# Four-visit turns behind the woven visits of a graph-attention edge pass, with buffer counts in registers

## The reference, cut to what matters

```python
xl = x @ Wl.T + bl
xr = x @ Wr.T + br
e = edge_attr @ We.T
m = xl[src] + xr[dst] + e
score = jnp.where(m > 0, m, NEG_SLOPE * m) @ att
smax = jax.ops.segment_max(score, dst, num_segments=N)
es = jnp.exp(score - smax[dst])
denom = jax.ops.segment_sum(es, dst, num_segments=N)
out = jax.ops.segment_sum(alpha[:, None] * xl[src], dst, num_segments=N)   # alpha = es / denom[dst]
```

## Time and profile before

| what | value |
|---|---|
| three timed runs, us | 6142.74, 6151.49, 6149.81 |
| median, us | 6149.81 |
| the profiled execution, us | 6128.16 |
| its span, us | 6126.2 |
| TensorE matmul busy | 5403.3 us, 88% |
| VectorE busy | 4183.1 us, 68% |
| GpSimd busy | 3068.8 us, 50% |
| ScalarE busy | 2663.4 us, 43% |
| indirect gathers (line 701) | 3200 |
| matmuls of the weighted sum (line 976) | 6352 |

### The profile page before, as it was taken

One profiled execution on the slowest core, in us unless ns is written; L12 is line 12 of the kernel. 1 busy time (PEld: TensorE's weight loads), 2 busy tenths in 40 slices (PEclk: granted clock), 3 DMA queues, 4 the chain that ended last, 5 costly groups with the idle time before them and its releaser, 6 DMA issues. The chain is left out here.

```text
span 6126.2 us, 174836 instructions
## 1 busy us (share of the span) xinstructions
PE 5403.3 (88%) x41112; PEld 3782.6 (62%) x41113; DVE 4183.1 (68%) x13187; ACT 2663.4 (43%) x5435; POOL 3068.8 (50%) x3217
## 2 busy tenths in 40 slices
PE   0599999999999976999999999999688899995998
PEld 0466666666666655666666666666587333334988
DVE  5677777777777776777777777777623788885121
ACT  0244444444444433444444444444311688883010
POOL 0477777777777755777777777777300000000000
PEclk9899999999999988999999999999888999997999
DMA  1344444444444434444444444444184233332967
GB/s 50 84 108 107 109 110 109 109 106 104 108 107 110 109 68 102 110 110 109 110 110 104 105 109 110 110 110 109 42 330 184 90 114 105 119 101 113 381 251 302
DMA packets 708090, 771.75 MB, mean 126 GB/s; under 512 B 376370, under 2 KB 629401, under 8 KB 682913
## 3 DMA queue, kind: packets, MB, share of 16 engines
q1 hardware_dynamic: 560771, 578.84, 31.2%
q0 software_dynamic: 102400, 105.06, 9.3%
q10 hardware_dynamic: 44832, 86.76, 3.9%
HBM read 678.16 MB, written 88.81 MB: 125 GB/s over the span
## 5 line engine op out<-in xcount | busy, mean ns | idle before, releaser
L701 POOL DMA_INDIRECT gat_rows<-rows_scr,gat_idx x3200 | 3056.2, 955 | 1214.2 <-issue 1035.0
L853 ACT ACTIVATE gat_weightsT<-gat_tps 128x512 f32<-128x512 f32 x800 | 477.7, 597 | 1146.5 <-PE gat_tps L967 1130.9
L839 ACT ACTIVATE gat_weights<-gat_masked,gat_newtop 128x512 f32<-128x512 f32 x800 | 577.4, 722 | 864.0 <-DVE gat_newtop L799 668.0
L746 DVE TENSOR_SCALAR adj_hot_key<-adj_iota_key,adj_winbase,adj_key 128x392 bf16<-128x392 int16 x2416 | 951.4, 394 | 0.2 <-issue 0.2
L957 PE MATMUL gat_sps<-gat_relu,gat_att 128*128 128x256 f32 x3200 | 906.3, 406 | 0.0
L915 PE MATMUL gat_counts<-adj_hot_key,adj_hot_lo 128*128 128x392 bf16 x2416 | 724.5, 334 | 153.0 <-DVE adj_hot_key L746 61.2
L745 DVE TENSOR_SCALAR adj_hot_lo<-adj_iota_lo,adj_low 128x128 bf16<-128x128 int16 x2416 | 672.1, 278 | 206.1 <-issue 184.6
L976 PE MATMUL gat_aps<-gat_rows,gat_weightsT 128*128 128x65 f32 x6352 | 797.5, 269 | 0.0
L976 PEld LDWEIGHTS gat_aps<-gat_rows,gat_weightsT 128*128 128x128 f32 x6352 | 771.9, 192 | 0.0
L915 PEld LDWEIGHTS gat_counts<-adj_hot_key,adj_hot_lo 128*128 128x128 bf16 x2416 | 232.7, 96 | 685.3 <-DVE adj_hot_key L746 493.7
L957 PEld LDWEIGHTS gat_sps<-gat_relu,gat_att 128*128 128x128 f32 x3200 | 543.4, 189 | 178.7 <-issue 137.3
(11 more groups left out here) (336 smaller groups left out, 6807.9 us busy)
## 6 DMA issues: line engine op xcount, KB each, us to landing
gcn_sum_adj<-adj_scr SPq DMA_DIRECT2D x98, 1568.0 KB, 8.5
gat_dstb<-dst_scr SPq DMA_DIRECT2D x800, 128.0 KB
gat_ea<-in_ea SPq DMA_DIRECT2D x800, 128.0 KB
gin_sum_adj<-adj_scr SPq DMA_DIRECT2D x49, 1568.0 KB, 8.5
adj_scr<-adj_tiles ACTq DMA_DIRECT2D x48, 1568.0 KB
at_adj<-adj_scr SPq DMA_DIRECT2D x84, 896.0 KB
gat_rows<-rows_scr,gat_idx POOLq DMA_INDIRECT x3200
gat_xr<-xr_scr SPq DMA_DIRECT2D x1600, 24.0 KB
```

The source lines that it names most:

```text
L701: pool.indirect_dma_start(rows[:, u, c, 0:ROW], None, rows_d, bass.IndirectOffsetOnAxis(ap=idx[:, u, c:c + 1], axis=0)).then_inc(s_g[u], 16)
L746: dve.tensor_scalar(plan.hot_key[:, slot, :], plan.iota_key[:], plan.winbase[:, bass.ds(w, 1)], plan.key[:, bass.ds(c, 1)], ALU.add, ALU.i ...
L839: act.activation(wts[:, j, :], masked[:, j, :], ACT.Exp, bias=newtop[:, j:j + 1], scale=-1.0)
```

## The change

Behind the 392 woven visits, the work is done in turns of four visits, not eight. `turns_sb` now holds the number of these short turns, (visits + 4 + 3 - 392) >> 2. SyncE and GpSimd get a second loop for them, and all five engines loop over it. The ring of eight slots stays, so behind the woven visits only slots 0 to 3 are used, and the visit that held a slot before is eight back in the first short turn and four back in any later one. SyncE and GpSimd keep the count to wait for in a register (`freed`), which grows by eight after the first short turn and by four after later ones. TensorE's weighted sum lags by three visits, so in the first three visits of a short turn it reads a slot given by a register (`behind`): 5 to 7 in the first short turn, 1 to 3 in later ones. VectorE reads the destinations of a plain visit from a fixed slot.

```diff
@@ -47,6 +47,7 @@
 WOVEN = NW // 2 // RING
+TAIL = WOVEN * RING
@@ -376,12 +377,12 @@  (visit_list)
-            dve.tensor_scalar(turns_f[:, 0:1], ends[:, NGP - 1:NGP], float(DRAIN + RING - 1), None, ALU.add)
+            dve.tensor_scalar(turns_f[:, 0:1], ends[:, NGP - 1:NGP], float(DRAIN + TURN - 1 - TAIL), None, ALU.add)
...
-            dve.tensor_scalar(turns_sb[:], cols_i[:, 0:1], RING.bit_length() - 1, None, ALU.arith_shift_right)
+            dve.tensor_scalar(turns_sb[:], cols_i[:, 0:1], TURN.bit_length() - 1, None, ALU.arith_shift_right)
@@ -645,11 +646,14 @@  (SyncE)
-            turns = sp.value_load(turns_sb[0:1, 0:1], min_val=2, max_val=VTAB // RING)
+            tails = sp.value_load(turns_sb[0:1, 0:1], min_val=1, max_val=(VTAB - TAIL) // TURN)
...
-            with sp.Fori(1, turns) as i:
+            with sp.Fori(1, WOVEN) as i:
                 for u in range(RING):
                     load_pair(i, u)
                     sp.wait_ge(s["message"], count("message", i * RING + u, RING))
                     group_parts(u)
                     range_parts(u)
+            freed, gone = sp.alloc_register(tag + "_sp_freed"), sp.alloc_register(tag + "_sp_gone")
+            sp.reg_mov(freed, count("message", TAIL, RING))
+            sp.reg_mov(gone, RING)
+            with sp.Fori(0, tails) as i:
+                for u in range(TURN):
+                    load_pair_at(i * (TURN // 2) + TAIL // 2, u)
+                    sp.wait_ge(s["message"], sp.snap(freed, min_val=1, max_val=1 << 16) + u)
+                    group_parts(u)
+                    range_parts(u)
+                sp.reg_add(freed, freed, gone)
+                sp.reg_mov(gone, TURN)
@@ (GpSimd)
-            with pool.Fori(0, turns) as i:
+            def gather(summed, u, filled):
+                pool.wait_ge(s_id[u], filled * 32 + 32)
+                pool.sem_inc(s_loaded, 1)
+                pool.wait_ge(s["sum"], summed)
+                pool.nop(nofuse=True)
...
+            with pool.Fori(0, WOVEN) as i:
                 for u in range(RING):
...
+                    gather(count("sum", i * RING + u, RING), u, i)
+            freed, gone = pool.alloc_register(tag + "_pool_freed"), pool.alloc_register(tag + "_pool_gone")
+            pool.reg_mov(freed, count("sum", TAIL, RING))
+            pool.reg_mov(gone, RING)
+            with pool.Fori(0, tails) as i:
+                for u in range(TURN):
+                    gather(pool.snap(freed, min_val=1, max_val=1 << 16) + u, u, i + WOVEN)
+                pool.reg_add(freed, freed, gone)
+                pool.reg_mov(gone, TURN)
@@ (VectorE)
-                    near = dstb[:, bass.ds((i & 1) * TURN + u, 1), :].rearrange("p a e -> p (a e)")
+                    near = dstb[:, bass.ds((i & 1) * TURN + u, 1), :].rearrange("p a e -> p (a e)") if woven else dstb[:, u, :]
...
-            with dve.Fori(WOVEN * RING // TURN, dve.snap(turns * (RING // TURN), min_val=1)) as i:
-                turn(i, False)
+            with dve.Fori(0, tails) as i:
+                turn(i + TAIL // TURN, False)
@@ (ScalarE)
-            with act.Fori(WOVEN, turns) as i:
-                for u in range(RING):
-                    visit(i * RING + u, u)
+            with act.Fori(0, tails) as i:
+                for u in range(TURN):
+                    visit(i * TURN + (TAIL + u), u)
@@ (TensorE)
             def turn(i, woven, first=False):
-                for u in range(RING):
-                    step = i * RING + u
+                visits(i * RING, RING, i, woven, first)
+
+            def visits(first_step, many, filled, woven, first=False, back=None):
+                for u in range(many):
+                    step = first_step + u
...
-                    j, v = (u - 3) % 2, (u - 3) % RING
+                    j = (u - 3) % 2
+                    v = slice((u - 3) % RING, (u - 3) % RING + 1) if back is None or u >= 3 else bass.ds(back + u, 1)
...
                     for c in range(GC):
-                        last = pe.matmul(aps[:, 0:D + 1], wtsT[:, j, c * P:(c + 1) * P], rows[:, v, c, 0:D + 1],
+                        last = pe.matmul(aps[:, 0:D + 1], wtsT[:, j, c * P:(c + 1) * P],
+                                         rows[:, v, c, 0:D + 1].rearrange("p a f -> p (a f)"),
                                          start=(c == 0), stop=(c == GC - 1))
...
-            with pe.Fori(WOVEN, turns) as i:
-                turn(i, False)
+            behind = pe.alloc_register(tag + "_pe_behind")
+            pe.reg_mov(behind, RING - 3)
+            with pe.Fori(0, tails) as i:
+                visits(i * TURN + TAIL, TURN, i + WOVEN, False, back=pe.snap(behind, min_val=TURN - 3, max_val=RING - 3))
+                pe.reg_mov(behind, TURN - 3)
```

More of the change, by code:

```diff
@@ L647, in _, with load_pair_at @@
             half = [sp.alloc_register(f"{tag}_half{j}") for j in range(2)]
-            turns = sp.value_load(turns_sb[0:1, 0:1], min_val=2, max_val=VTAB // RING)
+            tails = sp.value_load(turns_sb[0:1, 0:1], min_val=1, max_val=(VTAB - TAIL) // TURN)
+            def load_pair_at(word, u):
+                if u % 2 == 0:
+                    sp.reg_load(pair, words[0:1, bass.ds(word + u // 2, 1)])
             def load_pair(i, u):
-                if u % 2 == 0:
-                    sp.reg_load(pair, words[0:1, bass.ds(i * (RING // 2) + u // 2, 1)])
+                load_pair_at(i * (RING // 2), u)
             def group_parts(u):
@@ L689, in _ @@
         @block.gpsimd
         def _(pool):
-            turns = pool.value_load(turns_sb[0:1, 0:1], min_val=1, max_val=VTAB // RING)
+            tails = pool.value_load(turns_sb[0:1, 0:1], min_val=1, max_val=(VTAB - TAIL) // TURN)
             pool.wait_ge(s_ones, 1)
             pool.wait_ge(s_rows_out, 16)
-            with pool.Fori(0, turns) as i:
-                for u in range(RING):
[L696 to L703, removed]
+            def gather(summed, u, filled):
[3 more added lines that the diff above has]
+                pool.nop(nofuse=True)
+                for c in range(GC):
+                    pool.indirect_dma_start(rows[:, u, c, 0:ROW], None, rows_d,
+                                            bass.IndirectOffsetOnAxis(ap=idx[:, u, c:c + 1], axis=0)
+                                            ).then_inc(s_g[u], 16)
@@ L731, in _ @@
             dve.wait_ge(s_tab, 16)
-            turns = dve.value_load(turns_sb[0:1, 0:1], min_val=1, max_val=VTAB // RING)
+            tails = dve.value_load(turns_sb[0:1, 0:1], min_val=1, max_val=(VTAB - TAIL) // TURN)
             carry = [dve.alloc_register(f"{tag}_t{j}") for j in range(DRAIN)]
@@ L830, in _ @@
             act.wait_ge(s_xr_out, 48)
-            turns = act.value_load(turns_sb[0:1, 0:1], min_val=1, max_val=VTAB // RING)
+            tails = act.value_load(turns_sb[0:1, 0:1], min_val=1, max_val=(VTAB - TAIL) // TURN)
             act.sem_inc(s_empty, 2)
@@ L904, in _ @@
             pe.wait_ge(s_set, 3)
-            turns = pe.value_load(turns_sb[0:1, 0:1], min_val=1, max_val=VTAB // RING)
+            tails = pe.value_load(turns_sb[0:1, 0:1], min_val=1, max_val=(VTAB - TAIL) // TURN)
             for sem in s_used:
@@ L938, in turn @@
                     pe.nop(nofuse=True)
[L939 to L940 removed]
+                    pe.wait_ge(s_ld[v], filled * 48 + 48)
+                    pe.wait_ge(s_g[v], filled * (16 * GC) + 16 * GC)
                     pe.nop(nofuse=True)
```

## The result

The kernel after takes 6098.58 us (median of four runs, 6093.73 to 6101.15), the kernel before beside it 6150.65 us (four runs, 6142.74 to 6153.92): ratio 0.9916 with a 95% interval of 0.9899 to 0.9933. The forecast was 6115.2 us in a range of 6106 to 6128; the measured time lies 7.4 us under that range. The two profiled executions, however, are 6093.73 and 6128.16 us, 34.4 us apart, where the sum said 34.6.

What follows compares the result with a forecast made beforehand. TensorE's 3.78 us step closes the first pass and GpSimd's gathers, 5.0 us a visit, the second. Gains 15.1 + 20.0 less 0.5 register work make 34.6 us; 6149.8 - 34.6 = 6115.2 us, range 6106 to 6128.

Steps and rivals of the forecast that it cites:

- the sum: Gain over both passes: 15.1 + 20.0 - 0.5 = 34.6 us, against the profiled execution's 6128.2 us.
- Number of visits, 3168 gathers, 6288 sums: Both passes: one short turn each, 396 visits a pass for 400, so 3168 gathers and 6288 matmuls of the sum.
- First pass, 15.1 us, TensorE closes: End of first pass: four visits fewer bring TensorE's last sum 15.1 us earlier, and TensorE still closes the pass.
- Second pass, 20.0 us, GpSimd closes by 1.0 us: End of second pass: GpSimd's last gather starts 19.99 us earlier; its drain still closes, 1.0 us behind TensorE; gain 20.0 us.
- I take that as fixed: End of both passes: GpSimd's drain ends 8.57 us after the end of its last gather, before and after the change.
- Register work on TensorE, 0.5 us in the first pass: Short turn's first three visits: register-addressed rows cost TensorE 0.5 us in the first pass, 0 in the second.
- Lower bound of the gain, 31.2 us: TensorE closes both passes with 0.9 us of register work in each: 15.1 + 17.9 - 1.8 = 31.2 us.
- Everything else within 2 us of its length: Outside the ends of the two passes: every other stretch keeps its length within 2 us.
- 6149.8 - 34.6 = 6115.2, range from 6106: Whole kernel: gain taken off the median of the runs, 21.7 us above the profiled execution; range 6106 to 6128 us.
- Rival, slow short turn: Short turn: registers break the overlap, plain visits take 5.0 us for 3.78; gain 25 us, time 6125; 10%.
- Rival, second short turn: End of each pass: with 393 visits or more two short turns run; 6150 us or up to 2 us more; 2%.
- Rival, the woven loop lies elsewhere: Second pass's woven loop: moved code costs one instruction read a turn, 49 x 0.96 = 47 us, time 6162; 4%.

Runs made afterwards that it cites:

- e8: Kernel after with one gather instead of four in each of the four short visits; 6092.56 us (one run).
- e1: The kernel before again, no edit; 6149.86 us (12 runs), ratio 1.0007.
- e2: The kernel after again, no edit, beside the kernel before on one chip; 6104.70 us (6 runs), ratio 0.9942.
- e16: The kernel after once more, unedited, on another chip, beside three visits in the short turn; 6104.00 us, ratio 0.9947.
- e3: Kernel after with four added to the count, so two short turns run, 400 visits a pass; 6210.63 us, ratio 1.0118 against the kernel before.
- e4: Kernel after with the short turn written out on all engines, constants for loops and registers; 6135.65 us, ratio 0.9979 against the kernel before.
- e13: Kernel after with the short turn written out on all engines in the first pass only; profiled span 6115.0 us.
- e15: Kernel after with three visits in the short turn instead of four; 6106.62 us, ratio 0.9952 against the kernel before.
- e6: Kernel after with VectorE's short turn alone written out; 6104.44 us (one run).

## Why the prediction was right or wrong, point by point

- *Number of visits, 3168 gathers, 6288 sums*: right.
- *First pass, 15.1 us, TensorE closes*: right; 14.4 and 15.6 in two pairs.
- *Second pass, 20.0 us, GpSimd closes by 1.0 us*: the size came out (20.1, 20.5), in part by luck. GpSimd's drain ends 7.3 us behind its last gather, not 8.57, and TensorE and GpSimd tie (e8). "I take that as fixed" was wrong, and the prediction had named it as a sign of being wrong. The 1.3 us show: behind the 389th sum the second pass is 21.4 us shorter (42.0 to 20.6; 22.4 between e1 and e2). But its woven part is 1.3 us longer (1.9), which brings the total back to 20.1.
- *Register work on TensorE, 0.5 us in the first pass*: 0; the step is 3.78 as before, and the step into the plain loop is 4.01 (e16: 4.14) where it was 4.12.
- *Lower bound of the gain, 31.2 us*: a slip that changed nothing. 17.9 us is how much earlier TensorE ends, but GpSimd had closed that pass 3.0 us later. With TensorE closing, the pass gains 4369.4 - 4348.4 - 0.9 = 20.1 us, and the bound is 34.3. The step to line 1004 is 3.9 us by its own rows, not 3.8.
- *Everything else within 2 us of its length*: wrong. The rest behind the second pass took 1748.5 to 1754.7 us or 1766.1 to 1770.1, with one kernel (before) in both groups, by the moment at which the clock falls in the GIN's linear layers.
- *6149.8 - 34.6 = 6115.2, range from 6106*: this is the step that failed. The sum was made against an execution of 6128.2 and set off from a median of three runs 21.7 us above it, because "the removed visits are as good as empty in either". They are; but the 21.7 us look like a long draw of the untouched stages, mostly of the GIN's, and the kernel after drew anew. Against its own execution the sum gives 6128.2 - 34.6 = 6093.6, and the profiled execution of after took 6093.73. That it comes within 0.2 us is luck, too: the profiles of e1 and e2 are 48.6 us apart. The kernel before's later medians on ordinary chips were 6149.86 and 6144.25 (one chip), 6134.23 (one run), 6135.81 and 6139.80; less 34.6 they give 6100 to 6115. The kernel after's were 6098.58, 6104.70 and 6104.00, all under 6106. Of the first comparison's 52 us, only the profiled pair's 34.4 is explained stage by stage. That the other 17 are the same scatter is argued, from e1, e2 and e16 and from the granted clocks, not shown, as those runs weren't profiled. The range gave the draw 9 us below and should have given it about 20.
- *Rival, slow short turn*: refuted, 3.78 us a step.
- *Rival, second short turn*: not taken here, and mispriced by over 60 us (e3).
- *Rival, the woven loop lies elsewhere*: all but absent in this change (1949.2 for 1947.9, 1950.3 for 1948.4), but e4, e13 and e15 show that the danger was real, up to 20 us in place of 47, and not by the mechanism that was priced. The prediction watched for instruction packets; e4's second woven stretch has 3, as before's, and e13's has 2.
## What to carry to other kernels

Price a removed iteration by the step of the engine that closes its stage and check who is next; and price the case in which a shorter ring runs twice, since re-use after four slots, with the lower clock that the waiting brought, made a step 3.6 times as long. Set a forecast off from the same execution that the sum was made against, and let the range cover the spread of the stages that are not touched. After an edit ahead of a hot loop, measure the untouched loop too: its place alone moved it by up to 1%.

## What the runs showed that I had not expected

- A woven loop's length depends on where its code lies: 1949.2 to 1969.3 us for the same 388 steps of the second pass. The difference sits at fixed steps of the loop: in e6 the second, fourth, sixth and eighth of eight steps are 0.06 to 0.13 us longer than in e16, and the others up to 0.05 us shorter. Why is open.
- TensorE's granted clock fell to 0.50 in the middle of a busy stretch (e4: 32, then 24 matmuls in 8 us where after has 47), 5.8 to 26.7 us behind the start of the same matmuls in four executions.
- On one chip of five, SyncE's register instructions stalled by 0.5 us and more, some 800 times a pass, VectorE's some 200 times, and the same program took 7520 us.
- GpSimd's drain ended 6.3 (e8), 7.3 (after; 8.1 in e2's first pass) and 8.6 us (before, and e3) behind the end of its last gather.
